# Layer norm that keeps no transposed rows, normalised on GpSimd, with part of the preparation moved into the routing

## The reference, cut to what matters

```python
xn = (x - mean(x)) / sqrt(var(x) + 1e-5)              # per row of 256
dt = softplus(xn @ dt_w + dt_b)                       # 256 channels
b, c = xn @ B_w.T + B_b, xn @ C_w.T + C_b             # 32 states each
h[t] = exp(A * dt[t]) * h[t-1] + (dt[t] * xn[t]) * b[t]   # 256 channels x 32 states, A = -exp(log_A)
attn[t] = sum over states of h[t] * c[t] + D_skip * xn[t]
logits = xn @ wg                                      # 8 experts
idx, gates = the two best of softmax(logits), gates made to sum to 1
loc = running position of a row in its expert's list; a row past 4096 is dropped
ffn = sum over k of gates[k] * (relu(xn @ w1[e] + b1[e]) @ w2[e] + b2[e]),  e = idx[k], hidden 1024
out = x + attn + ffn
```

## Time and profile before

| what | us |
|---|---|
| median of 3 runs (3788.45 to 3792.91) | 3790.76 |
| profiled execution, first to last instruction | 3791.2 |
| DVE busy, share of the span | 3645.0, 96% |
| POOL busy | 3268.7, 86% |
| PE busy | 3217.7, 85% |
| ACT busy | 2563.4, 68% |

### The profile page before, as it was taken

The page is one execution under the profiler, slowest core; times in us unless marked ns, Lnnn a source line. Parts: engine busy times, 40 slices in busy tenths (PEclk is TensorE's granted clock), DMA queues, the critical chain, the costliest instruction groups (busy, mean ns, idle before and its releaser), DMA issues.

```text
span 3791.2 us, 64134 instructions
## 1 busy us (share of the span) xinstructions
PE 3217.7 (85%) x16548; PEld 2095.7 (55%) x16548; DVE 3645.0 (96%) x2281; ACT 2563.4 (68%) x4811; POOL 3268.7 (86%) x1722
## 2 busy tenths in 40 slices
PE   7776888888888888888888888888888888888887
PEld 4354555555555555555555555555555555555554
DVE  6787999999999999999999999999999999999998
ACT  3245677667776777767776777767776777677775
POOL 0017999999999999999999999999999999999996
PEclk9898999999999999999999999999999999999998
DMA  9974555555656556565656555465656555565666
GB/s 326 340 122 151 158 165 164 166 142 157 170 159 184 165 156 170 140 165 161 171 163 185 160 158 161 136 183 156 175 159 181 163 160 143 147 188 158 167 169 163
DMA packets 345249, 644.98 MB, mean 170 GB/s; under 512 B 49405, under 2 KB 221441, under 8 KB 344641
## 3 DMA queue, kind: packets, MB, share of 16 engines
q1 hardware_dynamic: 252018, 538.77, 44.1%
q0 software_dynamic: 67776, 85.24, 14.1%
q10 hardware_dynamic: 25104, 16.91, 2.0%
HBM read 515.55 MB, written 142.80 MB: 174 GB/s over the span
## 4 chain that ended last, share of the span: by engine, by line
DVE 36%; issue 28%; PE 9%; POOL 9%; ACT 8%; DMA 6%; DVEq 2%; SPq 1%; ACTq 0%; POOLq 0%
DVE hc L1215 18%; DVE h L1226 15%; POOL u L1027 5%; ACT bank L798 3%; DMA dt<-dt_rows 2%; PE bank L494 2%; PE bank L648 2%; PE bank L639 2%; POOL out_rows L985 2%; DMA dt<-x 2%; ACT xgt L802 1%; ACT za L766 1%; DVE dt_n L1131 1%; POOL xg L973 1%; ACT bank L868 1%
## 5 line engine op out<-in xcount | busy, mean ns | idle before, releaser
L1027 POOL TENSOR_TENSOR u<-dtx,b_sb 128x1024 f32<-128x1024 f32 x1024 | 2515.4, 2530 | 120.7 <-DVE h L1226 85.3
L1226 DVE TENSOR_TENSOR_SCAN h<-bank,u 128x1024 f32<-128x1024 f32 x1024 | 2301.8, 2279 | 17.4 <-POOL u L1027 11.5
L798 ACT ACTIVATE bank<-dt,a_neg 128x1024 f32<-128x1024 f32 x1026 | 1129.8, 1108 | 378.3 <-DVE h L1226 305.0
L639 PE MATMUL bank<-xgt,w_sb 128*128 128x256 f32 x4096 | 1027.9, 394 | 245.5 <-ACT ht L840 219.3
L1215 DVE TENSOR_TENSOR hc<-h,bank 128x2048 f32<-128x2048 f32 x514 | 1165.2, 2267 | 34.4 <-ACT bank L868 33.0
L639 PEld LDWEIGHTS bank<-xgt,w_sb 128*128 128x128 f32 x4096 | 745.6, 192 | 619.1 <-issue 536.2
L648 PE MATMUL bank<-w_sb,ht 128*128 128x256 f32 x4096 | 954.1, 387 | 26.0 <-ACT o_sb L855 24.6
L648 PEld LDWEIGHTS bank<-w_sb,ht 128*128 128x128 f32 x4096 | 774.4, 193 | 224.6 <-issue 125.3
L840 ACT ACTIVATE ht<-bank,b_sb 128x256 f32<-128x256 f32 x1024 | 423.6, 463 | 280.0 <-PE bank L639 279.9
L598 PE MATMUL bank<-hc,rsum 128*32 128x512 f32 x4112 | 549.3, 606 | 2.9 <-DVE hc L1215 2.9
L985 POOL DMA_INDIRECT out_rows<-o_sb,sidx x258 | 415.6, 1611 | 55.8 <-issue 34.5
(11 more groups left out here) (114 smaller groups left out, 1819.0 us busy)
## 6 DMA issues: line engine op xcount, KB each, us to landing
b_sb<-bc_rows SPq DMA_DIRECT2D x258, 512.0 KB
c_sb<-bc_rows SPq DMA_DIRECT2D x258, 512.0 KB, 4.0
dt<-dt_rows SPq DMA_DIRECT2D x132, 512.0 KB, 8.0
dtx<-dtx_rows SPq DMA_DIRECT2D x132, 512.0 KB, 5.2
w_sb<-w SPq DMA_DIRECT2D x18, 1024.0 KB
dt_rows<-dt_n SPq DMA_DIRECT2D x137, 128.0 KB
dtx_rows<-dtx_n SPq DMA_DIRECT2D x137, 128.0 KB
out_rows<-y_sb POOLq DMA_DIRECT2D x34, 512.0 KB
```

The source lines that it names most:

```text
L639: mm = pe.matmul(m_ps[:, c, :], w1_sb[:, kk, ch * P:(ch + 1) * P], xgt[:, kk, :], start=(kk == 0), stop=(kk == KD - 1))
L798: act.activation(a_ps[k % 2], dt[:, k % GPP, :], ACT.Exp, scale=a_neg[:, col:col + 1]).then_inc(a_ready, 1)
L1027: pool.tensor_tensor(u[:, k % UB, :], dtx[:, gp, :], b_sb[:, j, :], ALU.mult).then_inc(u_ready, 1)
L1226: dve.tensor_tensor_scan(h[:, k, :], a_ps[k % 2], u[:, k % UB, :], 0.0, ALU.mult, ALU.add).then_inc(scan_done, 1)
```

## The change

- Layer norm: `xnt_d` is gone with its stores and loads. DVE does statistics and reciprocal only; POOL normalises (`normalise`), ACT evacuates a turned group into `xnt` itself. The groups are taken in the order 4 to 31, 0 to 3, so that the last four (sequences 0 and 1) stay in `xnt`.
- Logits: PE uses the turned rows as the stationary side and `wg` (8 columns) as the moving one, so tokens are on partitions at once.
- Steps: each loads 128 rows of `xn_rows` (SP, `load_rows`), turns them on PE (`turn_rows`, two transposes into the PSUM bank of the experts), and ACT copies them into `xnt` (`rows_turned`). In place of that the load of a half of `xnt` is gone.
- Routing: preparation 0 stands ahead of the first count, preparation 1 ahead of the second; in the loop turn q does preparation q + 2. None is left after the loop.
- SP loads the first dt, dtx, b and c tiles when the stores of preparations 0 to 7 have landed, before it stores preparations 8 and 9, and before `map_ready`.
- POOL clears the half of `h` that DVE cleared after `map_ready`.

```diff
-            with sp.Fori(0, NGRP // U - 1) as ii:
+            with sp.Fori(0, NGRP // U - 2) as ii:
                 for r in range(U):
-                    rows_out(ii * U + r, r)
-                    load_x(r, ii * U + r + U)
+                    rows_out(ii * U + r, ii * U + r + U, r)
+                    load_x(r, ii * U + r + 2 * U)
...
-            load_xnt(0, 0)
-            load_xnt(1, 1)
+            def load_rows(buf, seq, q):
+                sp.dma_start(xr[:, buf, :], xn_d[bass.ds(seq * S + q * Q, Q), 0:D]).then_inc(xr_in[buf], 16)
+
+            load_rows(0, 1, 3)
...
-            sp.wait_ge(bcv_done, NG + 1)
-            store_bc(NG, 1, 0)
-            store_dt(NG, 1, 0)
-            store_dtx(NG, 1, 0)
-            sp.wait_ge(bcv_done, NG + 2)
-            store_bc(NG + 1, 1, 1)
-            sp.wait_ge(base_out, 16 * NBASE)
-            sp.wait_ge(xnt_in, 32)
-            sp.wait_ge(b_st, 16 * (NG + 2) + 1)
-            sp.wait_ge(dt_st, 16 * (NG + 1) + 1)
-            sp.wait_ge(dtx_st, 16 * (NG + 1) + 1)
-            sp.wait_ge(map_ready, 1)
+            sp.wait_ge(b_st, 16 * NG + 1)
+            sp.wait_ge(dt_st, 16 * NG + 1)
+            sp.wait_ge(dtx_st, 16 * NG + 1)
+            sp.wait_ge(dtx_free, 1)
             for gp in range(GPP):
                 load_dt(0, 0, gp)
                 load_dtx(0, 0, gp)
...
             load_b(1, 1)
             load_c(0, 0)
+            sp.wait_ge(bcv_done, NG + 1)
+            store_bc(NG, 1, 0)
...
+            sp.wait_ge(map_ready, 1)
             sp.wait_ge(gates_out, 16)
...
-                        src = xnt_d.rearrange("k p t -> p k t")[:, gh, bass.ds((b + 2) % B * S, S)]
-                        sp.dma_start(xnt[:, bo, gh, :], src).then_inc(xnt_in, 16)
...
                     store_dtx(NG + 1 + st, seq1 % 2, q1)
+                    sp.wait_ge(fill_done, st * FS + 1)
+                    settle(sp)
+                    load_rows((s + 1) % 2, (b + 1 + (s % SPS + 4) // NG) % B, (s % SPS + 4) % NG)
                     next_c(1)
...
             for k in range(2):
+                prep(k, 0, k)
                 count(k)
                 if k == 0:
                     pe.wait_ge(gate_out, 1)
...
+                    def turn_rows():
+                        pe.wait_ge(xr_in[s % 2], 16 * (e * (SPE // 2) + st_e // 2 + 1))
+                        free(XF)
+                        for kk in range(KD):
+                            mm = turn(x_ps[:, kk, :], xr[:, s % 2, kk * P:(kk + 1) * P], True)
+                        mm.then_inc(fill_done, 1)
...
                     quad(1)
+                    turn_rows()
                     pe.wait_ge(xg_in, 16 * SJ * (st + 2))
...
+            first_prep(0)
+            act.wait_ge(gate_in, 3)
+            act.activation(e2, e2, ACT.Exp).then_inc(setup_act, 1)
+            act.wait_ge(setup_act, 3)
+            first_prep(1)
+
+            act.wait_ge(gates_ready, 1)
+            act.dma_start(xn_d[:, D:D + 2].rearrange("(i p) d -> p i d", p=P), gates[:]).then_inc(gates_out, 16)
...
                     if o == 0:
-                        evac_prep(q)
-                        act.wait_ge(v_done, q + 1)
+                        evac_prep(q + 2)
+                        act.wait_ge(v_done, q + 3)
...
                             up_out(3)
+                            rows_turned()
...
+            def normalise(pos, ii, r):
+                pool.wait_ge(rstd_done, pos + 1)
...
+                for j in range(G):
+                    ins = pool.tensor_scalar(xn[:, r, j, :], xt_in[:, r, j, :], mv[:, r % 2, j, 0:1],
+                                             rstd[:, r % 2, j:j + 1], ALU.subtract, ALU.mult)
+                ins.then_inc(xn_done, 1)
...
+            prep_dt(0)
             tot = bank[:, 2:4, :].rearrange("p b c -> p (b c)").rearrange("p (i e) -> p i e", e=E)
...
+            dve.sem_inc(dtx_free, 1)
+            prep_dt(1)
             dve.wait_ge(setup_act, 3)
             link(dve.tensor_scalar(mx[0], e2, 1.0, None, ALU.add))
...
-                prep_dt(q)
-            prep_dt(NG)
-            prep_dt(NG + 1)
+                prep_dt(q + 2)
```

More of the change, by code:

```diff
@@ L142, in ssm_moe @@
         dtx_n = sb("dtx_n", [P, KD, Q])
-        xnt_out = b_sb[:].rearrange("p a (k t) -> p a k t", k=KD)
+        xnt_part = [xnt[:, i // 2, :, i % 2 * G * P:(i % 2 + 1) * G * P] for i in range(U)]
+        xr = sb("xr", [P, 2, D])
         y_t = sb("y_t", [P, 2, HALF])
@@ L165, in ssm_moe @@
         m_ps = bank[:, 7, :].rearrange("p (c s) -> p c s", s=SL)
+        x_ps = bank[:, 7, 0:KD * P].rearrange("p (k t) -> p k t", k=KD)
         map_ps = bank[:, 4, :]
@@ L183, in ssm_moe @@
         xn_out = [sem(f"xn_out{i}") for i in range(U)]
-        xnt_st = [sem(f"xnt_st{i}") for i in range(2)]
+        xr_in = [sem(f"xr_in{i}") for i in range(2)]
         base_out = sem("base_out")
@@ L564, in count, with map_batch @@
                 mm.then_inc(pe_route, 1)
+            def map_batch(n, o):
+                pe.wait_ge(oh_ready, n + 1)
+                pe.wait_ge(low_ready, n + 1)
+                for r in range(OHB):
+                    i, k = r // 2, r % 2
+                    pe.matmul(map_low, oh_low[:, o % 2, i, :, k], oh_c[:, o % 2, i, :, k],
+                              start=False, stop=True, skip_group_check=True)
+                    mm = pe.matmul(map_high, oh_high[:, o % 2, i, :, k], oh_c[:, o % 2, i, :, k],
+                                   start=False, stop=True, skip_group_check=True)
+                mm.then_inc(oh_used, 1)
+            pe.wait_ge(weights_in, 16 * 7)
             for k in range(2):
+                prep(k, 0, k)
                 count(k)
@@ L739, in _ @@
             act.mul(a_neg[:], a_neg[:], -1.0).then_inc(setup_act, 1)
-            act.wait_ge(gate_in, 3)
-            act.activation(e2, e2, ACT.Exp).then_inc(setup_act, 1)
-            act.wait_ge(setup_act, 3)
-            act.wait_ge(gates_ready, 1)
-            act.dma_start(xn_d[:, D:D + 2].rearrange("(i p) d -> p i d", p=P), gates[:]).then_inc(gates_out, 16)
             def evac_z(p):
@@ L948, in _ @@
         def _(pool):
-            start_at_one(pool, u_ready, prep_done)
+            start_at_one(pool, u_ready, prep_done, xn_done)
             pool.memset(o_sb[:], 0.0).then_inc(zeroed, 1)
             pool.memset(y_sb[:], 0.0).then_inc(zeroed, 1)
+            def normalise(pos, ii, r):
+                pool.wait_ge(rstd_done, pos + 1)
+                settle(pool)
+                pool.wait_ge(xn_out[r], 16 * ii + 1)
+                settle(pool)
+                pool.wait_ge(turned, pos - U + 1 + TURNED0)
+                settle(pool)
+                for j in range(G):
+                    ins = pool.tensor_scalar(xn[:, r, j, :], xt_in[:, r, j, :], mv[:, r % 2, j, 0:1],
+                                             rstd[:, r % 2, j:j + 1], ALU.subtract, ALU.mult)
+                ins.then_inc(xn_done, 1)
+            with pool.Fori(0, NGRP // U) as ii:
+                for r in range(U):
+                    normalise(ii * U + r, ii, r)
+            pool.wait_ge(turned, NGRP + TURNED0)
+            for r in range(U):
+                pool.wait_ge(xn_out[r], 16 * (NGRP // U) + 1)
+            pool.memset(h[:, GPP:2 * GPP, :], 0.0).then_inc(zeroed, 1)
             def dtx_part(p, par, q):
@@ L1051, in _ @@
         def _(dve):
[L1052 removed]
+            start_at_one(dve, hc_done, dt_done)
             seq = [0]
@@ L1218, in _ @@
             dve.memset(y_ps.rearrange("p b c -> p (b c)"), 0.0).then_inc(nsum_done, NSUM0)
-            dve.memset(h[:, GPP:2 * GPP, :], 0.0).then_inc(scan_done, SCAN0)
+            dve.wait_ge(zeroed, 3)
+            dve.sem_inc(scan_done, SCAN0)
             with dve.Fori(0, STEPS) as st:
```

200 lines of the change are left out of this document (88 added, 112 removed).

## The result

The changed kernel takes 3900.39 us (median of 4 runs, 3893.55 to 3909.36) against 3790.54 (3788.45 to 3792.91): ratio 1.0287, 95% interval 1.0266 to 1.0309. It is slower; I had said 3766, range 3739 to 3792. The profiled execution has a span of 3907.7 us. The experiments further down are one execution each where no number of runs is given.

The account below looks back on a forecast made before the run. The prediction took DVE to bound the steps and bytes to bound layer norm. First scan at 113.9 + 167 + 14.2 = 295.1 instead of 322.0, steps +2: 25 less than 3791.2, so 3766 us, range 3739 to 3792.

Parts of the forecast that it names:

- neither decides any more: Layer norm: with less work on PE and ACT, neither would set the group period, forecast at 3.2 us.
- That stage is bound by bytes.: Layer norm: DMA share 1.03 at 336 GB/s; 1.05 MB instead of 1.57 MB a group would take 3.0 us.
- the 42 us: Layer norm: its end for DVE would come 42.4 us earlier, at 113.9 instead of 156.3 us.
- I take 2.1: Layer norm: POOL's four tensor_scalar of a group would take 2.1 us, between bounds of 0.9 and 3.0.
- rival B: Layer norm: POOL sets the period, 4.1 us if DVE locks it out, or 4.5; time 3797 or 3811; chance 0.14.
- first wait: Routing, before the gates: DVE waits 17 us as preparation 0's store lies behind the copy of x in SP's queue.
- second 13.98: Routing, last loop turn: ACT held 11 us because preparation 8's store stands behind twelve loads in SP's queue.
- M - T: Routing, from layer norm's end for DVE to the map being ready: 167 us forecast against 148.5 before.
- Rival A: Routing: SP's queue doesn't hold the stores; 3738 to 3740 us, or 3755 with only the second wait missing; chance 0.17.
- M to F: From the map being ready to the first scan: 14.2 us forecast against 17.2, with POOL's first gather waiting less.
- +2: Steps: extra DMA, PE's transposes and ACT's copy would add 2 us in all, range -3 to +8.
- Rival C: Steps: ACT's copy and the bank handshake delay c_copy(3) by 0.2 us a step, 26 us, time 3791; chance 0.08.

Follow-up runs that it names:

- l_dve: Changed kernel with all four tensor_scalar of a group back on DVE instead of POOL, the new logits kept; 3905.7 us.
- l_both: Changed kernel with DVE normalising and the logits as before the change, only the stores of turned rows gone from layer norm; 3892.96 us.
- r_sp: Changed kernel, SP's queue reordered: half the copy of x issued inside the loop, preparation 8's stores ahead of the first tile loads; 3881.44 us.
- s_join: Changed kernel with rows turned into the free half of moe_down(0)'s bank under its semaphore, copied just ahead of down_out(0); 3833.85 us.
- f_b4: Changed kernel with s_join's turning, r_sp's queue, DVE normalising, next group's statistics ahead of the root wait, four extra bf16 products per group on PE; 3774.25 us.
- f_w512: Same kernel as f_b4, but one extra float32 product of 512 columns per group on PE instead of the four bf16 ones; 3815.7 us.
- f_b4p: f_b4 with POOL normalising again and DVE's statistics in their old order; 3864.22 us.
- s_late: Changed kernel with the rows turned ahead of moe_down(1) and copied ahead of down_out(1); 4539.69 us.

## Why the prediction was wrong, point by point

- *"PE loses the products with 512 columns and ACT a copy; neither decides any more."* This is the step that failed in layer norm. I took the logits for as long as a turn, 1.09. The sixteen products measured 3.42, and the turns went from 1.09 to 1.95, with TensorE at its lower level all through layer norm. PE decides: with POOL out of the way (l_dve) the period is still 5.01. 32 groups at 5.01 instead of 4.49 are 16.6 of the 22.3 us; the other 5.7 lie at the ends, where PE is late with the last group (DVE waits 15.13 us there, before 6.35). I never looked at how full PE was: busy 129.22 of 151 us in the earlier trace rows.
- *"That stage is bound by bytes."* True in part, and worth much less than the 42 us that I took from it. A DMA share of 1.03 says that the queues were full; who waits for them, and what stands right behind, I didn't ask. DVE waited 24.2 us for loads, and its own list, at 4.1 us a group, was next. With DVE normalising a third fewer bytes (l_both, share 0.76) left the period where it was; in the changed kernel no engine waits for bytes, PE is full at 5.01.
- *"I take 2.1"* for POOL's four: 4.85. I interpolated between a memset and a product of two tensors, 3.0 us for four; the instruction is 1.6 times as dear as the dearer of them. It takes 1217 to 1220 ns in all of 17 instructions from 98.8 to 118.9 us, with DVE at work beside some of them, so rival B's mechanism (DVE locking POOL out) does not show; its second price, 1.1 us for one, was nearly the size. Its place was second in line: POOL at 4.85 lies just under PE at 5.01. (B's two times should have been 3796 and 3809 by its own terms, for 3797 and 3811.) The Trainium skill, "GPSIMD Engine Reference", section 4.1, has one-input operations at roughly line rate, an estimated 0.2 us here; the trace has 1.21 and decides.
- *Routing*: first wait 12.05 (17 forecast), second 13.98 (11), M - T 162.4 (167). The mechanism holds, and r_sp shows the cause. Rival A is out. M to F was 15.3 (14.2), POOL's first gather waited 1.93 instead of 5.96.
- *Steps, "+2"*: +82.3. I counted work (0.3 and 0.4 us) and looked for cover at one place, `c_copy(3)`. I had seen the new wait on both sides, but priced it as the sum of its instructions. PE is 86% busy in a step and waits at that place as long as before, so `moe_down(0)` came late by the turn and ACT's copy, and everything behind it with it: ACT ahead of `down_out` (288.7 us of waits for 60.5), and by ACT's list the `c_copy` of the next step. Rival C had this end and put 26 us on it. s_join shows the hand-over as the cause, 74 us between two traces and 46 to 82 by all of them; how much of it is the clock's stays open.

## What to carry to other kernels

A full DMA share is not yet a price: ask who waits for a transfer, and how long that engine's own list is, before you count on fewer bytes. Price a new hand-over between two in-order engines by what stands ahead of it in each list, and look first for an existing semaphore that it can share: here 86 us became 11.5. Price a stretch of TensorE that is rebuilt at both levels of its clock, and read the level from the time of an instruction that you know.

## What the runs showed of the hardware

- Eight 128x128 float32 turns: 1.09 us at TensorE's upper level, 1.95 at the lower. Sixteen products of 8 columns with a weight load each: 1.85 and 3.42. In the changed kernel PE was busy without a pause from its first groups on and yet at the lower level to the end of layer norm (T 178.6). With four bf16 products of 512 columns more in each group the level was up from 18.2 us and the period 3.8 us instead of 5.0 (f_b4); with one float32 product of 512 columns it was up only from 118.5 us (f_w512).
- A POOL tensor_scalar of 128x256 float32 with two per-partition scalars takes 1.21 us (12 in a row 14.48, f_b4p).
- Sixteen float32 products of 256 columns: 3.62 us in a row with other work (s_join), 5.22 behind a pause of 1.84 (before), 5.44 behind one of 4.40 (s_late).
